# Graph attention layer, score stage: scores from rows with sums on VectorE, a split root, another order and fills from SyncE

## What is computed

```python
h = relu(layernorm(x))
Q, K, V = h @ Wq, h @ Wk, h @ Wv                      # [N, 8, 32] each
scores = einsum('ehd,ehd->eh', Q[dst], K[src]) * 32 ** -0.5
w = softmax of scores over the edges with the same dst
out = zeros.at[dst].add(V[src] * w) @ Wo_w + Wo_b
out = layernorm(h + out) * ln1_g + ln1_b
ffn = gelu(out @ ffn_w1 + ffn_b1) @ ffn_w2 + ffn_b2
x = x + layernorm(out + ffn) * ln2_g + ln2_b
```

## Time and profile before

| | |
|---|---|
| median of 3 runs | 1871.33 us (1869.89 to 1872.53) |
| profiled execution | 1869.43 us |
| its span, first to last instruction | 1867.7 us |
| score stage | 0 to 357.7 us |
| softmax stage | 357.7 to 406.2 us |
| message stage | 406.2 us to about 578 us |
| node stage | about 578 us to the end |

### The profile page before, as it was taken

The page is one execution under the profiler, slowest core; times in us unless marked ns, Lnnn a source line. Parts: engine busy times, 40 slices in busy tenths (PEclk is TensorE's granted clock), DMA queues, the critical chain, the costliest instruction groups (busy, mean ns, idle before and its releaser), DMA issues.

```text
span 1867.7 us, 29784 instructions
## 1 busy us (share of the span) xinstructions
PE 1684.7 (90%) x9846; PEld 1411.2 (76%) x9846; DVE 1471.2 (79%) x4479; ACT 1288.1 (69%) x2340; POOL 1337.4 (72%) x1342
## 2 busy tenths in 40 slices
PE   0999999639961599999999999999999999999997
PEld 0677777418741488888888888888888888888887
DVE  3565665367732599999999999999999999999996
ACT  1677777302210688888888888888888888888884
POOL 7777774007772777877887787778778877877783
PEclk9999999859985799999999999999999999999999
DMA  3778887313434577777776777777777767776761
GB/s 104 238 258 267 267 262 221 122 57 97 136 105 148 106 167 170 168 170 170 165 172 167 175 158 174 167 170 168 169 170 167 171 166 174 158 175 166 172 132 57
DMA packets 132414, 309.41 MB, mean 166 GB/s; under 512 B 14022, under 2 KB 68214, under 8 KB 132260
## 3 DMA queue, kind: packets, MB, share of 16 engines
q0 software_dynamic: 42624, 139.33, 37.2%
q1 hardware_dynamic: 37492, 115.61, 18.3%
q10 hardware_dynamic: 52144, 52.56, 8.5%
HBM read 140.66 MB, written 118.20 MB: 139 GB/s over the span
## 4 chain that ended last, share of the span: by engine, by line
PE 66%; DMA 1%; DVE 1%; POOL 0%; ACT 0%; SPq 0%; issue 0%; DVEq 0%; POOLq 0%; ACTq 0%
PE d_F L991 30%; PE d_Y L1002 30%; PE d_T L978 5%; DMA d_fb_row<-in_fb 1%; DMA d_z<-agg_scratch 0%; PE d_Y L968 0%; ACT d_zn L903 0%; PE d_F L961 0%; SPq L727 0%; POOL d_zx_rstd L788 0%; POOL d_u L775 0%; POOL d_u L773 0%; ACT d_z L914 0%; DVE d_y_stats L847 0%; DVE d_zx_stats L860 0%
## 5 line engine op out<-in xcount | busy, mean ns | idle before, releaser
L1002 PE MATMUL d_Y<-d_w_hi,d_act_hi 128*128 128x256 f32 x1568 | 458.5, 292 | 0.0
L1002 PE MATMUL d_Y<-d_w_hi,d_act_lo 128*128 128x256 f32 x1568 | 441.8, 282 | 0.0
L1002 PE MATMUL d_Y<-d_w_lo,d_act_hi 128*128 128x256 f32 x1568 | 441.7, 282 | 0.0
L903 ACT ACTIVATE d_zn<-d_z,d_zx_nmr,d_zx_rstd 128x256 f32<-128x256 f32 x392 | 224.3, 596 | 149.1 <-POOL d_zx_nmr L791 149.1
L991 PE MATMUL d_F<-d_zt_hi,d_w_hi 128*128 128x512 f32 x784 | 321.5, 410 | 2.1 <-DVE d_zt_lo L823 1.4
L991 PE MATMUL d_F<-d_zt_hi,d_w_lo 128*128 128x512 f32 x784 | 310.2, 396 | 0.0
L991 PE MATMUL d_F<-d_zt_lo,d_w_hi 128*128 128x512 f32 x784 | 310.0, 395 | 0.0
L923 ACT ACTIVATE d_F<-d_F,d_fb_col 128x512 f32<-128x512 f32 x392 | 259.5, 662 | 61.5 <-PE d_F L991 61.4
L773 POOL TENSOR_TENSOR d_u<-d_zn,d_g_row 128x1024 f32<-128x1024 f32 x98 | 293.5, 2995 | 6.0 <-ACT d_zn L903 6.0
L1002 PEld LDWEIGHTS d_Y<-d_w_hi,d_act_lo 128*128 128x128 f32 x1568 | 296.1, 189 | 0.0
L1002 PEld LDWEIGHTS d_Y<-d_w_lo,d_act_hi 128*128 128x128 f32 x1568 | 295.9, 189 | 0.0
(11 more groups left out here) (159 smaller groups left out, 3538.5 us busy)
## 6 DMA issues: line engine op xcount, KB each, us to landing
agg_scratch<-a_bias_row ACTq DMA_DIRECT2D x50, 1024.0 KB, 6.7
d_x<-in_x SPq DMA_DIRECT2D x98, 512.0 KB, 4.1
d_z<-agg_scratch POOLq DMA_DIRECT2D x98, 512.0 KB, 5.6
d_x<-d_b_wide POOLq DMA_DIRECT2D x98, 512.0 KB, 7.5
out<-d_o SPq DMA_DIRECT2D x98, 512.0 KB, 2.9
c_cont<-cont_scratch SPq DMA_DIRECT2D x25, 256.0 KB, 3.4
a_xd<-in_x,a_idx POOLq DMA_INDIRECT x100, 2.8
a_xs<-in_x,a_idx POOLq DMA_INDIRECT x100, 4.7
```

The lines of the kernel that those rows point to most:

```text
L903: ins = nc.scalar.activation(zn[gz % 2][:, j, :], z[gz % ZR][:, j, :], ACT.Identity, bias=zx_nmr[:, at % NR, 0, j:j + 1], scale=zx_rstd[:, ...
L1002: ins = nc.tensor.matmul(Y[s % 2][:, j, :], a[:, c, j * P:(j + 1) * P], w[:, c, :], start=False, stop=(c == KF - 1 and w is w2_lo), skip_g ...
```

## The change

It touches `score_stage` alone. The four parts of the name are all in the one diff.

- q and k are computed as rows: the activations are the stationary operand, the weights the moving one (256 columns), edges lie on partitions. The products of a group are `[128 edges, 4 tiles, 256]`; VectorE sums them over each head's 32 features into `cols` (128 by 32), TensorE transposes that to 32 by 128, ScalarE scales it, and four DMAs store it. v is computed as before. `head_of` is gone.
- 1/sqrt(variance + eps) comes from a square root on ScalarE, a reciprocal on VectorE and one Newton step of three operations there, in place of the power on GpSimd.
- The steps begin at -2 instead of -3. VectorE serves the statistics of group s + 2, and up to step 0 it does them after the products and low parts. On ScalarE the last two normalisations of side 1 move to the next step, between the key copies. TensorE runs 40 matmuls (`WARM`) on loaded weights before its first group.
- The fills are issued by SyncE, two in each step ahead of its wait for the scores; the bias load too.

```diff
-        head_of = sb("a_head_of", [P, KD, H])
...
+        cols = [sb(f"a_cols{r}", [P, GT * H]) for r in range(2)]
...
-        FIRST = -3
+        WARM = 40
+        FIRST = -2
...
             @block.sync
...
+                sp.dma_start(bias_row[:], wo_b.broadcast_to([P, D])).then_inc(bias_in, 16)
+                sp.wait_ge(bias_in, 16)
...
+                for s in range(EG):
+                    for n in range(2 * s, 2 * s + 2):
+                        sp.dma_start(table[n], bias_row[:].rearrange("p (r d) -> p r d", r=1)
+                                     .broadcast_to([P, FR, D])).then_inc(filled, 16)
+                    sp.wait_ge(s_out, s + 1)
+                    for j in range(GT):
+                        sp.dma_start(score_dram[:, bass.ds(s * GR + j * P, P)], score[s % 2][j * H:(j + 1) * H, :])\
+                          .then_inc(stored[s % 2], 16)
...
             @block.gpsimd
...
-                    nc.gpsimd.tensor_tensor(rstd[:, r], veps[:, r], mhalf[:], ALU.pow).then_inc(rstd_done, 1)
...
             @block.vector
...
+                    nc.vector.reciprocal(rstd[:, r], std[:, r]).then_inc(guess_done, 1)
...
+                    nc.vector.tensor_tensor(square[:, r], rstd[:, r], rstd[:, r], ALU.mult).then_inc(square_done, 1)
...
+                    nc.vector.scalar_tensor_tensor(square[:, r], square[:, r], -0.5, veps[:, r], ALU.mult, ALU.mult)\
...
+                    nc.vector.scalar_tensor_tensor(rstd[:, r], square[:, r], 1.5, rstd[:, r], ALU.add, ALU.mult)\
...
+                def head_sums(s):
...
+                    dve.wait_ge(prod_done, 2 * s + 2)
+                    if s >= 2:
+                        dve.wait_ge(s_done, s - 1)
+                    nc.vector.tensor_reduce(cols[s % 2][:], prod[:].rearrange("p j (h d) -> p (j h) d", h=H), AX.X, ALU.add)\
...
+                for s in range(FIRST, EG):
+                    if s <= 0:
+                        products(s)
+                        head_sums(s)
+                        low_part(s + 1, 0)
+                        low_part(s + 1, 1)
+                        statistics(s + 2)
+                        inverse_root(s + 2)
+                    else:
+                        statistics(s + 2)
+                        products(s)
+                        head_sums(s)
+                        low_part(s + 1, 0)
+                        inverse_root(s + 2)
+                        low_part(s + 1, 1)
...
             @block.scalar
...
+                for s in range(FIRST, EG):
+                    key_copy(s, 0)
+                    normalise(s + 1, 1, (2, 3))
+                    key_copy(s, 1)
+                    high_part(s + 1, 0)
+                    if s >= 1:
+                        root(s + 2)
+                    value_copies(s)
+                    high_part(s + 1, 1)
+                    if s <= 0:
+                        root(s + 2)
+                    score_copy(s)
+                    normalise(s + 2, 0, (0, 1, 2, 3))
+                    normalise(s + 2, 1, (0, 1))
...
             @block.tensor
...
+                for n in range(WARM):
+                    nc.tensor.matmul(T[:, n % KD, 0:D], w_hi[0][:, 0, 0:P], w_hi[0][:, 0, :], start=True, stop=True)
...
+                def rows_by(out, n, side, j):
...
+                    for k in range(KD):
+                        for p, (w, a) in enumerate(((w_hi, ht_hi), (w_lo, ht_hi), (w_hi, ht_lo))):
+                            ins = nc.tensor.matmul(out, a[side][:, k, at], w[n][:, k, :],
...
-                        for k in range(KD):
-                            ins = nc.tensor.matmul(S[0:H, :], head_of[:, k, :], prod[:, k, :],
-                                                   start=(k == 0), stop=(k == KD - 1))
...
+                        nc.tensor.transpose(S[0:GT * H, 0:P], cols[s % 2][:], ident[:]).then_inc(s_done, 1)
```

More of the change, by code:

```diff
@@ L249, in _, with statistics @@
-                for c in range(FIRST, EG):
-                    step(Step(c))
+                def statistics(g):
+                    if not there(g):
+                        return
+                    r = g % 4
+                    for side in range(2):
+                        dve.wait_ge(gathered[side][r], 16 * GT * (g // 4 + 1))
+                        for j in range(GT):
+                            nc.vector.bn_stats(stats[:, r, side, j, :], xg[side][r][:, j, :]).then_inc(stats_done, 1)
+                    for side in range(2):
+                        for j in range(GT):
+                            dve.wait_ge(stats_done, 2 * GT * g + GT * side + j + 1)
+                            ins = nc.vector.bn_aggr(mv[:, r, side, j, :], stats[:, r, side, j, :])
+                    ins.then_inc(mv_done, 1)
+                    dve.wait_ge(mv_done, g + 1)
+                    nc.vector.tensor_scalar(veps[:, r], mv[:, r, :, :, 1], LN_EPS, None, ALU.add).then_inc(veps_done, 1)
@@ new lines, in products @@
+                def products(s):
+                    if not there(s):
+                        return
+                    for c in range(2):
+                        at = slice(2 * c, 2 * c + 2)
+                        dve.wait_ge(k_out, 2 * s + c + 1)
+                        dve.wait_ge(q_done, 2 * s + c + 1)
+                        nc.vector.tensor_tensor(prod[:, at, :], Q[:, at, :], ksb[:, at, :], ALU.mult).then_inc(prod_done, 1)
+                def head_sums(s):
+                    if not there(s):
+                        return
+                    dve.wait_ge(prod_done, 2 * s + 2)
+                    if s >= 2:
+                        dve.wait_ge(s_done, s - 1)
+                    nc.vector.tensor_reduce(cols[s % 2][:], prod[:].rearrange("p j (h d) -> p (j h) d", h=H), AX.X, ALU.add)\
+                        .then_inc(cols_done, 1)
@@ new lines, in low_part @@
+                def low_part(g, side):
+                    if not there(g):
+                        return
+                    for c in range(KD):
+                        dve.wait_ge(hi_done[side], KD * g + c + 1)
+                        nc.vector.tensor_tensor(ht_lo[side][:, c, :], T[:, c, :], ht_hi[side][:, c, :].bitcast(f32),
+                                                ALU.subtract).then_inc(lo_done[side], 1)
+                for s in range(FIRST, EG):
[13 more added lines that the diff above has]
+                        low_part(s + 1, 1)
@@ new lines, in value_copies, with root @@
+                def value_copies(s):
+                    if there(s):
+                        for c in range(KD):
+                            act.wait_ge(v_done, KD * s + c + 1)
+                            nc.scalar.copy(vt[:, c, bass.ds(s * GR, GR)], V[c]).then_inc(v_out, 1)
+                def root(g):
+                    if there(g):
+                        act.wait_ge(veps_done, g + 1)
+                        nc.scalar.activation(std[:, g % 4], veps[:, g % 4], ACT.Sqrt).then_inc(std_done, 1)
@@ L311, in project, with features_by @@
+                def features_by(out, n, side, c):
                     for k in range(KD):
```

252 lines of the change are left out of this document (98 added, 154 removed).

## The result

The changed kernel takes 1828.13 us (median of 4 runs, 1827.0 to 1829.66); beside it the kernel before takes 1870.87. The ratio is 0.9772, with a 95% interval of 0.9757 to 0.9786: 42.7 us faster. The forecast was 1840 within 1824 to 1855, a gain of 31. Sign and range held; the size was a quarter short.

The account below looks back on a forecast made before the run. TensorE was taken to set the 12.18 us period. Start 10.9 + 22 periods 21.6 + end 0.7 - table load 1.3 = 31.9 us off the 1867.7 span: 1835.8, 1839.4 as a median, say 1840; range 1824 to 1855.

Parts of the forecast that it names:

- The period's mechanism: Score stage, each group: TensorE's second transposes wait for VectorE's low part behind the reduction; period 11.2 us, 0.98 saved.
- the forecast of 0.73: Score stage: TensorE's new stall ahead of the second transposes, 0.73 us in every group, of 1.70 us removed.
- q and k as rows: Score stage, TensorE: 48 matmuls of 256 columns at 0.119 us, 5.7 us as now; bounds -0.1 and +0.2 a group.
- The start: First groups of the score stage: third group's q at 66 instead of 76.9 us; gain 10.9 us, bounds 5 and 14.
- the step that credits the new order of the first groups: Start of the score stage: group 0 served before group 1's statistics, first q at 31 us (45.92 before).
- The exponential's load: Softmax stage, ScalarE: a table load of 1.28 us after the wait, before the exponential; +1.3 us.
- What was moved at no cost: Score stage: fills moved to SyncE and 40 opening matmuls on TensorE, both taken at nothing.
- Transfers bind: Rival, score stage: transfer engines can't hold more than about 0.83 busy, period 11.7 us, 1851 us; chance 0.11.
- The clock falls: Rival, score stage: each new stall lowers TensorE's clock, period 13.8 us, 1897 us; chance 0.04.
- No stall: Rival, score stage: copy or reduction quicker, or VectorE reads sooner; period 10.5 us, 1825 us; chance 0.12.
- The table is reloaded: Rival, score stage: 2 x 1.28 us more on ScalarE in every group, period near 11.7, 1851 us; chance 0.03.
- nothing itself: Score stage, GpSimd: the power goes, 9.9 us of gathers remain, running ahead until the ring of four stops it; no gain.

Follow-up runs that it names:

- e6: The changed kernel with the head sums put behind the low part of side 0 in VectorE's steady steps: 1816.82 us.
- e7: The changed kernel with the reduction over the heads done twice, first into a spare tile: 1859.18 us.
- e10: The kernel before with one digit changed, VectorE's statistics serving group s + 2 instead of s + 3: 1858.97 us.
- e2: The changed kernel with the steady order from the first step, no branch for steps up to 0 on VectorE and ScalarE: 1822.75 us.
- e1: The changed kernel with the fills and the bias load issued by ScalarE again: 1828.96 us.
- e3: The changed kernel without the 40 opening matmuls (WARM = 0): 1828.16 us.
- e4: The changed kernel with the root back as a power on GpSimd, between the sixth and seventh gather: 1851.16 us.
- e5: The kernel before with only the root moved to ScalarE (square root) and VectorE (reciprocal, Newton step): 1869.76 us, ratio 0.9995.
- e8: The kernel e6 with the first two fills moved from the first step to the second: 1815.3 us.

## Why the prediction was right, and where it was off

- **The period's mechanism.** Right: TensorE waits 0.31 us ahead of the second transposes, released by the low part behind the reduction, in every steady group; e6 and e7 show it from both sides. **The size** was off by 0.32 us a group, 7 of the 9 us that are missing in the span: counted by starts, as the forecast of 0.73 was, the stall is 0.48 us. Its links, from the first q: second key copy at 6.03 (forecast 6.1), product 6.64 to 7.33 (6.78 to 7.47), reduction to 8.59 (8.7), low part to 9.78 (10.0), second transposes at 9.93 (10.13), next q at 10.86 (11.2). The product starts 0.04 after the copy's end, not 0.09. The low part starts 0.09 before the reduction ends, as independent instructions of VectorE overlap. Transposes, sums' transpose and the turn to q take 0.93, where I had 0.96 + 0.12: the transpose of the sums has its own start only 0.03 us ahead of q's.
- **The reduction.** 1.22 us, as interpolated.
- **q and k as rows.** 0.119 us a matmul (149.49 to 149.61 and on). From the first q to the first transposes it is 5.78 us, 0.07 more than before and inside the bounds.
- **The start.** The forward working put the third group's q at 66; it was 62.3, from steps of 16.2 us instead of 17 and an allowance of 1 us for the lower clock that wasn't needed. The gain of 14.6 us lies just outside the term's own bounds of 5 and 14; only the range of the whole covered it. The time was worked forward in the order that the kernel has, so it isn't luck that it came near, but the reason given was wrong: the step that credits the new order of the first groups. The nearer statistics (s + 2 instead of s + 3) give 11.4 of the 14.6 us when they are changed alone (e10), and the branch costs 5.4 us of the total (e2). I had read the cause in the trace rightly, statistics of later groups ahead of group 0, and gave it to the wrong lines of the diff: both lines of it change what stands ahead, and I didn't work the steady order forward for comparison.
- **The exponential's load.** I put 1.28 us behind the wait; it stands at the stage's start, 313.94, in time that ScalarE has free for 21 us. I had taken the place from the first load, which follows its wait in both traces; why this one precedes its wait, no trace shows.
- **What was moved at no cost.** The fills on SyncE (e1) and the opening matmuls (e3) give and cost nothing in the medians, as said. For the fills this is two effects at the start that cancel, of which the prediction had one, the fills beside the first gathers (18.0 taken, 17.41 measured); it didn't see that the gathers would start 1.9 us earlier.
- **Rivals.** *Transfers bind* is out: 0.96 busy in e6 at a period of 10.35. *The clock falls* is out: 1.00 in every steady stretch with 0.31 us stalls, and still in e7 with 1.5 us ones (150 to 200 us). Only in e4, with waits up to 2.5 us, do stretches of 50 us have 0.97 (200 to 250). *No stall* would have been e6, for which the forecast of 10.5 us a group was 0.15 too high. *The table is reloaded* is out: the trace has three loads in all.
- **GpSimd.** The prediction says of the power's removal that it gives nothing itself. For the kernel before that holds (e5). In the changed kernel it is worth 23 us (e4), 18 of them since 8 gathers and a power are 11.7 us and the period is 10.88, and the rest at the start. "Nothing itself" should have been followed by what it is worth once the other part is in. The reason beside it, that GpSimd runs ahead until the ring of four stops it, isn't what the trace before shows: between 70 and 280 us GpSimd waits there for no buffer, but for the variance from VectorE ahead of its power, 15 times and 7.5 us in total. In the changed kernel the ring stops it only from 185 us on, since 8 gathers take 10.0 us of the 10.88.

The Trainium skill, ScalarE: Activation LUTs, section What ACT_TABLE_LOAD costs, adds a drain to each switch. The trace after speaks against it again: the load of 19.65 ends at 20.93 and the square root starts at 20.94, and the load in the node stage starts at 591.76, 0.01 us after the activation before it, and ends 0.01 us ahead of the next at 593.05.

## What to carry to other kernels

Two engines that are both within a few per cent of the period hide each other: work out for each part of a change what it gives alone and what it gives once the other is in, because here next to nothing and 20 us alone became 43 together. When work moves to an engine with time to spare, ask what stands behind it in that engine's order and who waits for that; the same reduction one place later was worth 11 us. In a pipeline's first steps every instruction that waits for later groups' data holds up the first group's, so try the lead itself before an order of its own for the start, and work both forward.

## What the runs showed of the hardware

- Idle times of TensorE of much the same length gave different clocks: after 3.30 us idle (before) eight transposes took 1.94 us, after 3.02 us (changed kernel, 55.17) they took 1.09 and after 3.09 us (e1, 55.24) 1.97, and after 2.29 us they took 1.06 in the changed kernel and 1.94 in e3. The length of the wait alone didn't decide in these traces.
- The matmuls of q and k at 256 columns and those of v at 512 take nearly the same time per column: their starts are 0.119 and 0.234 us apart, with a weight load before each.
- The transfer engines moved 309 to 314 GB/s for 50 us and more (e6) with gathers of 1 KB rows and fills side by side, where the kernel before had 257, and VectorE waited for no gather between 70 and 280 us.
- The index load of 100 KB landed 2.1 us after its issue in the changed kernel, where the bias load is issued at 2.74, and 4.0 and 4.3 us after it in the kernel before and in e1, where the bias load is issued beside it at 0.80. The first gather started at 3.20, 5.06 and 5.36 us.
- A gather issued at 12.72 us beside two fills of 1 MB landed 4.7 us later (changed kernel); without fills beside it the eighth gather landed 2.8 us after its issue (e1, e8).
